# Layer 2's time mixing as a pipeline of four parts instead of two halves

## The reference

```python
h = layer_norm(x, ln1_g, ln1_b)
k = time_shift(h, mix_k) @ Wk_t.T
v = time_shift(h, mix_v) @ Wv_t.T
r = jax.nn.sigmoid(time_shift(h, mix_r) @ Wr_t.T)
wkv_out, new_state = wkv(-exp(time_decay), time_first, k, v)
x = x + r * wkv_out                      # time mixing
h2 = layer_norm(x, ln2_g, ln2_b)
kc = time_shift(h2, cmix_k) @ Wk_c.T     # 128 -> 512
rc = jax.nn.sigmoid(time_shift(h2, cmix_r) @ Wr_c.T)
vv = jnp.square(jax.nn.relu(kc)) @ Wv_c.T
x = x + rc * vv                          # channel mixing
```

## Time and profile before

| | |
|---|---|
| timed runs | 2173.11, 2174.31, 2175.66 us; median 2174.31 |
| profiled execution | 2182.17 us, span 2180.4 us |
| TensorE, VectorE, ScalarE, GpSimd busy | 1875.8 (86%), 1526.5 (70%), 1310.5 (60%), 588.6 us (27%) |
| chain that ended last | PE 52%, DVE 28%, ACT 8% |

### The profile page before, as it was taken

How to read it: one execution, slowest core, us unless ns; L and a number is a source line. 1 busy time by engine, 2 the same in 40 slices (tenths; PEclk the granted TensorE clock), 3 DMA queues, 4 the chain that set the end, 5 groups by cost and what they waited for, 6 DMA issues and landing times.

```text
span 2180.4 us, 37976 instructions
## 1 busy us (share of the span) xinstructions
PE 1875.8 (86%) x13416; PEld 1265.7 (58%) x13416; DVE 1526.5 (70%) x3631; ACT 1310.5 (60%) x2803; POOL 588.6 (27%) x569
## 2 busy tenths in 40 slices
PE   7999776997999999968977488999997997779886
PEld 4777564445777777644444254666665676534465
DVE  5777677866777677547848848899997456678533
ACT  5777533775878888735765656776665212357622
POOL 3223003102544443414001003444343001221043
PEclk9999997998999999978998699999999998889898
DMA  4000003411000000006302000000001000363202
GB/s 202 2 2 2 1 1 119 138 55 39 1 2 1 1 1 1 1 15 196 102 1 80 0 1 1 1 1 1 1 2 39 20 1 1 117 180 112 59 25 80
DMA packets 80156, 87.40 MB, mean 40 GB/s; under 512 B 6579, under 2 KB 70116, under 8 KB 79074
## 3 DMA queue, kind: packets, MB, share of 16 engines
q1 hardware_dynamic: 78625, 82.49, 11.9%
q0 software_dynamic: 1344, 2.49, 0.4%
HBM read 54.39 MB, written 30.70 MB: 39 GB/s over the span
## 4 chain that ended last, share of the span: by engine, by line
PE 52%; DVE 28%; ACT 8%; issue 6%; POOL 3%; DMA 2%; SPq 1%; DVEq 0%; POOLq 0%; ACTq 0%
PE bank L469 44%; DVE scratch L1269 4%; PE bank L653 2%; ACT XN L2059 2%; DVE scratch L3134 2%; DVE scratch L3154 2%; PE bank L3016 2%; PE bank L368 2%; PE bank L693 1%; DVE stats L245 1%; DVE XN L3174 1%; DVE scratch L1671 1%; DVE w_keep L1958 1%; ACT L2137 1%; PE bank L1238 1%
## 5 line engine op out<-in xcount | busy, mean ns | idle before, releaser
L469 PE MATMUL bank<-scratch 64*128 64x256 bf16 (+6 forms) x2936 | 307.7, 303 | 34.5 <-DMA scratch<-parts 13.5
L1269 DVE TENSOR_REDUCE scratch<-bank 128x2 f32<-128x512 f32 x384 | 243.1, 685 | 59.8 <-PE bank L469 59.2
L469 PE MATMUL bank<-w_keep,scratch 128*128 128x128 f32 (+4 forms) x1760 | 243.1, 329 | 19.2 <-DVE scratch L2001 4.0
L469 PEld LDWEIGHTS bank<-scratch 64*128 64x128 bf16 (+4 forms) x2936 | 177.3, 123 | 139.0 <-DVE scratch L1269 44.6
L1355 ACT ACTIVATE w_keep<-bank 128x512 f32<-128x512 f32 x384 | 212.4, 597 | 71.3 <-PE bank L469 63.6
L469 PE MATMUL bank<-XNT,w_keep 128*128 128x256 f32 (+4 forms) x800 | 236.9, 435 | 6.5 <-POOL w_keep L2198 5.5
L469 PEld LDWEIGHTS bank<-w_keep,scratch 128*128 128x128 f32 (+3 forms) x1760 | 181.7, 184 | 84.0 <-issue 54.8
L469 PE MATMUL bank<-w_early,scratch 64*128 64x256 f32 (+3 forms) x1152 | 163.3, 344 | 24.0 <-ACT w_early L3234 8.7
L469 PEld LDWEIGHTS bank<-XNT,w_keep 128*128 128x128 f32 x800 | 149.7, 196 | 58.0 <-issue 28.3
L469 PEld LDWEIGHTS bank<-w_early,scratch 64*128 64x128 f32 (+3 forms) x1152 | 119.0, 183 | 69.1 <-issue 28.5
L469 PE MATMUL bank<-w_keep 128*32 128x256 f32 (+2 forms) x1728 | 141.0, 389 | 13.3 <-ACT w_keep L1355 5.4
(11 more groups left out here) (461 smaller groups left out, 3852.0 us busy)
## 6 DMA issues: line engine op xcount, KB each, us to landing
scratch<-parts SPq DMA_DIRECT2D x24, 1024.0 KB, 5.2
parts<-scratch SPq DMA_DIRECT2D x192, 96.0 KB, 2.8
parts<-scratch SPq DMA_DIRECT2D x96, 64.0 KB, 2.1
w_early<-pack_l3f SPq DMA_DIRECT2D x1, 5206.0 KB, 15.4
w_keep<-pack_l2f SPq DMA_DIRECT2D x1, 2124.0 KB, 13.3
...
```

Source lines behind the costliest of these rows:

```text
L469: return pe.matmul(out, lhsT, rhs, start=start, stop=stop, skip_group_check=True)
L1269: dve.tensor_reduce(neg[:, :, h], self.compare_bank(g)[:, :].rearrange("p (t s) -> p t s", s=S), AXX, ALU.max, negate=True).then_inc(*s.ma ...
```

## The change

The pair of halves becomes a pipeline of four. A part has its own residual (`residual_dve`), moments (`moments_dve`, four tiles), norm (`norm_dve` and `norm_act`: two tiles scaled by each engine), turn (`turn_part_pe`) and affine step (`second_affine_dve`); the end of a quarter is `output_dve`. VectorE starts part 2's and part 3's first step later, and takes sums of a later part, weigh of the next, and gate of the current one in turn. ScalarE does the sigmoids of r in the middle of part 0's and part 1's work. TensorE makes the r products ahead of the v products of parts 1 to 3, and from there on turn, up, the next part's num, down for each part. The receptance sigmoids of quarters 0 and 1 are followed by one more load of the Ln and Exp table, and quarter 2's by one more load of the sigmoid table. The banks of num and turn are other ones.

The diff, cut to the functions and orders that the prediction speaks of:

```diff
@@ time_mixing @@
-    PARTS, FIRST, LAST = range(4), (0, 1), (2, 3)
-    num_bank = lambda part: k.bank[4 + part if part in FIRST else part]
+    PARTS = range(4)
+    num_bank = lambda part: k.bank[(4, 5, 2, 3)[part]]
+    turn_bank = lambda part: k.bank[(0, 3, 2, 3)[part]]
...
+    def norm_dve(dve, part):
+        tiles = slice(4 * part, 4 * part + 4)
+        total = k.moments[:, 1, tiles]
+        dve.wait_ge(*s.deviation.at("second", part))
+        dve.scalar_tensor_tensor(out=total, in0=total, scalar=-0.5, in1=k.rs[:, tiles], op0=ALU.mult, op1=ALU.mult).then_inc(*s.rstd.up("second", part))
+        dve.wait_ge(*s.rstd.at("second", part))
+        for i in range(4 * part, 4 * part + 2):
+            dve.tensor_scalar(O2[:, i], k.XN[:, i], k.rs[:, i:i + 1], k.moments[:, 1, i:i + 1], ALU.mult, ALU.add).then_inc(*s.normed.up("second", i))
...
@@ pe @@
...
-        for part in (0, 1):
-            num_pe(e, part)
-        turn_half_pe(e, "second", (0, 1))
-        e.wait_ge(*s.formed.at("second", 1))
-        up_pe(e, 0)
-        down_pe(e, 0)
-        num_pe(e, 2)
-        num_pe(e, 3)
-        up_pe(e, 1)
-        turn_half_pe(e, "later", (2, 3))
-        down_pe(e, 1)
-        e.wait_ge(*s.formed.at("later", 3))
-        for q in (2, 3):
+        for part in PARTS:
+            input_pe(e, part, 0)
+        input_pe(e, 0, 1)
+        for part in PARTS:
+            input_pe(e, part, 2)
+        for part in PARTS[1:]:
+            input_pe(e, part, 1)
+        num_pe(e, 0)
+        for q in PARTS:
+            turn_part_pe(e, q)
             up_pe(e, q)
+            if q + 1 in PARTS:
+                num_pe(e, q + 1)
             down_pe(e, q)
+
+    def input_pe(pe, part, n):
+        _, now, prev, _ = folded[INPUTS[n][0]]
+        bank, b0 = k.bank[part], part * PART
+        if n == 1:
+            pe.wait_ge(*s.stacked.at("in", part, 2 if part else 0))
+        elif n == 2:
+            pe.wait_ge(*s.stacked.at("in", part, 0 if part else 1))
...
@@ dve @@
...
+        ahead_dve(e, 0)
+        ahead_dve(e, 1)
+        sums_dve(e, 0)
+        raised_dve(e, 0)
+        ahead_dve(e, 2)
         level_dve(e, 0)
+        sums_dve(e, 1)
+        weigh_dve(e, 0)
+        whole_dve(e, 0)
+        raised_dve(e, 1)
+        gate_dve(e, 0)
+        ahead_dve(e, 3)
+        level_dve(e, 1)
+        residual_dve(e, 0)
         sums_dve(e, 2)
+        moments_dve(e, 0)
+        weigh_dve(e, 1)
+        norm_dve(e, 0)
+        whole_dve(e, 1)
+        second_affine_dve(e, 0)
...
+        residual_dve(e, 2)
+        moments_dve(e, 2)
         weigh_dve(e, 3)
+        norm_dve(e, 2)
+        whole_dve(e, 3)
+        second_affine_dve(e, 2)
+        gate_dve(e, 3)
+        output_dve(e, 0)
+        residual_dve(e, 3)
+        moments_dve(e, 3)
+        output_dve(e, 1)
+        norm_dve(e, 3)
+        second_affine_dve(e, 3)
+        output_dve(e, 2)
+        output_dve(e, 3)
@@ act @@
...
+        input_act(e, 0, 0)
+        input_act(e, 1, 0)
         weights_act(e, "first", 0)
+        input_act(e, 2, 0)
+        weights_act(e, "first", 1)
         input_act(e, 3, 0)
-        weights_act(e, "first", 1)
+        log_act(e, 0)
         input_act(e, 0, 1)
+        weights_act(e, "second", 0)
+        weights_act(e, "third", 0)
         weights_act(e, "first", 2)
...
         inverse_act(e, 0)
         for part in PARTS:
             input_act(e, part, 2)
         e.preload_act_table_set("natural_log_exp_and_others")
+        log_act(e, 1)
+        weights_act(e, "second", 1)
+        input_act(e, 1, 1)
+        weights_act(e, "third", 1)
+        norm_act(e, 0)
...
+        weights_act(e, "second", 3)
+        relu_act(e, 7)
+        norm_act(e, 2)
         weights_act(e, "third", 3)
         inverse_act(e, 3)
+        receptance_act(e, 0)
+        receptance_act(e, 1)
+        e.preload_act_table_set("natural_log_exp_and_others")
+        relu_act(e, 8)
+        relu_act(e, 9)
+        norm_act(e, 3)
+        relu_act(e, 10)
+        relu_act(e, 11)
+        receptance_act(e, 2)
```

More of the change, by code:

```diff
@@ L2625, in gate_dve, with residual_dve @@
         dve.tensor_tensor(num, num, r, ALU.mult).then_inc(*s.divided.up("gated", part))
[L2627 to L2642, removed]
+    def residual_dve(dve, part):
+        xn = k.XN[:, 4 * part:4 * part + 4, :]
+        dve.wait_ge(*s.rolled.at("num", part))
+        if part == 0:
+            dve.wait_ge(*s.scaled.at("outer", NT - 1))
+        dve.tensor_tensor(xn, xn, num_bank(part)[:, :].rearrange("p (j d) -> p j d", d=D), ALU.add).then_inc(*s.added.up("num", part))
+        dve.wait_ge(*s.added.at("num", part))
+        stats_dve(k, dve, "second", k.XN, range(4 * part, 4 * part + 4))
@@ new lines, in moments_dve @@
+    def moments_dve(dve, part):
+        tiles = slice(4 * part, 4 * part + 4)
+        m0, m1, v0, v1 = (k.stats[:, tiles, n] for n in (1, 4, 2, 5))
+        spread, total, var = (k.moments[:, n, tiles] for n in range(3))
+        dve.wait_ge(*s.stats.at("second", 4 * part + 3))
+        dve.tensor_tensor(spread, m0, m1, ALU.subtract).then_inc(*s.moments.up("spread", part))
+        dve.tensor_tensor(total, m0, m1, ALU.add).then_inc(*s.moments.up("total", part))
+        dve.tensor_tensor(var, v0, v1, ALU.add).then_inc(*s.moments.up("sums", part))
+        dve.wait_ge(*s.moments.at("spread", part))
+        dve.tensor_tensor(spread, spread, spread, ALU.mult).then_inc(*s.moments.up("square", part))
+        dve.wait_ge(*s.moments.at("square", part))
+        dve.scalar_tensor_tensor(out=var, in0=spread, scalar=P / 4, in1=var, op0=ALU.mult, op1=ALU.add).then_inc(*s.variance.up("second", part))
@@ new lines, in second_affine_dve, with output_dve @@
+    def second_affine_dve(dve, part):
+        dve.wait_ge(*s.turned.at("second", part))
+        dve.tensor_scalar(HT[:, 2 * part:2 * part + 2, 1:PADDED], turn_bank(part)[:, :].rearrange("p (b s) -> p b s", s=S), w["r_g2"], w["r_b2"],
+                          ALU.mult, ALU.add).then_inc(*s.formed.up("second", part))
+    def output_dve(dve, q):
+        tiles = k.X[:, 4 * q:4 * q + 4, :]
+        dve.wait_ge(*s.gated.at("rc", q))
+        dve.wait_ge(*s.multiplied.at("vv", q))
+        dve.tensor_tensor(RC[q % 2], RC[q % 2], k.bank[4 + q % 2][:, :], ALU.mult).then_inc(*s.vector.up("product", q))
+        dve.wait_ge(*s.vector.at("product", q))
+        dve.wait_ge(*s.pool.at("residual", q))
+        dve.tensor_tensor(tiles, tiles, RC[q % 2].rearrange("p (j d) -> p j d", d=D), ALU.add).then_inc(*s.added.up("out", q))
+        dve.wait_ge(*s.added.at("out", q))
+        stats_dve(k, dve, "next", k.X, range(4 * q, 4 * q + 4))
@@ L2696, in up_pe @@
             bank = k.bank[u % 2]
+            if g == 0:
+                pe.wait_ge(*s.formed.at("second", q))
             if u >= 2:
@@ L2759, in dve @@
-        affine_dve(e, "later", "r_g2", "r_b2", LAST)
-        for q in range(QUARTERS):
-            tiles = k.X[:, 4 * q:4 * q + 4, :]
-            e.wait_ge(*s.gated.at("rc", q))
-            e.wait_ge(*s.multiplied.at("vv", q))
-            e.tensor_tensor(RC[q % 2], RC[q % 2], k.bank[4 + q % 2][:, :], ALU.mult).then_inc(*s.vector.up("product", q))
-            e.wait_ge(*s.vector.at("product", q))
-            e.wait_ge(*s.pool.at("residual", q))
-            e.tensor_tensor(tiles, tiles, RC[q % 2].rearrange("p (j d) -> p j d", d=D), ALU.add).then_inc(*s.added.up("out", q))
-            e.wait_ge(*s.added.at("out", q))
-            stats_dve(k, e, "next", k.X, range(4 * q, 4 * q + 4))
+        residual_dve(e, 1)
```

118 lines of the change are left out of this document (48 added, 70 removed).

## The result

In nine runs the changed kernel took a median of 2185.32 us (2181.80 to 2190.07); nine runs of the kernel before on the same chip took 2175.66 (2171.66 to 2180.01). The ratio is **1.0045 (95% interval 1.0034 to 1.0056)**, 9.8 us slower (7.4 to 12.2). On the median of 2174.31 that the prediction started from, this is 2184.1 us.

A forecast was written before the change was run, and what follows sets the result against it. Two loads, TensorE's and VectorE's, stood one behind the other. Walking the in-order queues ended the stage at 1297.1 instead of 1290.45, 6.7 us longer; 2174.3 + 6.7 = 2181.0 us, range 2175.5 to 2187.5.

The forecast's parts named there:

- rival B: Clock also lost before value products and up 2, last up starting cold: +13.5, halved +10; 2184 to 2188 us; chance 0.16.
- r0: VectorE can add part 0's num at 1210.2, num queued behind value products that wait for sigmoids; 2.2 us lost.
- r1: VectorE can add part 1's num at 1230.3, after a cold first up of 9.2 us; 3.1 us lost.
- r2: VectorE can add part 2's num at 1246.3, after a warm up of 8.75 us with receptance; VectorE waits 2.7.
- r3: VectorE can add part 3's num at 1266.3, after warm up 2 (8.75) and relu 8's hold (1.3); 5.1 us waited.
- U3: Start of part 3's up, the last, on TensorE: 1282.1, behind down 2, turn and affine.
- Down 2: TensorE's second last down, waiting for squares until 1274.8 and starting cold: 5.9 us, all warm 3.7.
- The end: From residual 3 to last statistics: output 1, norm, relus 10 and 11, down 2, last up in series; ends 1297.1, before 1290.45.
- Rival A: TensorE warm throughout, up 0 and down 2 at high clock: 2.2 off twice, +2.3, 2176.6 us; chance 0.12.
- C: Engine loads set the end, VectorE's five waits (15.8 us) vanish: 2165.2 us, 0.4% faster; chance 0.08.
- Costs at nothing: 12 more small VectorE operations of the moments lie in its waits; without that cover 1 to 2 us.
- Table loads: On ScalarE, 1.29 us each up to the next operation, no drain; by the skill page some 4 us longer.

The follow-up runs named there:

- x5: Changed kernel with the old projection order on TensorE (k, v, r) and r products in banks 4 to 7: stage 114.0 us, ratio 1.0021.
- x3: Changed kernel plus matrix products nobody reads in TensorE's idle stretches (7 after num 0, 2 after turn 2, 8 after num 3): stage 110.6 us, ratio 1.0013.
- x1: Changed kernel with relu 10 and 11 ahead of norm 3 on ScalarE: stage 109.8 us, ratio 1.0014.
- x2: Changed kernel with quarter 1's output behind norm 3 and affine 3 on VectorE: stage 114.7 us, ratio 1.0031.
- x4: Changed kernel with the next part's num among the products of up on TensorE instead of behind them: stage 110.8 us, ratio 1.0004.
- x7: Changed kernel with the edits of x1, x2, x4 and x5 together: stage 99.5 us, ratio 0.9964.
- x9: x7 plus idle products after num 0 and turn 2, and ScalarE's third weights of part 3 between norm 2's root and scaling: stage 97.1 us, ratio 0.9958.

## Why the prediction was right, and what it mis-sized

The prediction was slower with 0.72, 2181.0 us, range 2175.5 to 2187.5: direction and range held. The size did not: it forecast +6.7 us, the stage shows +9.1 and the ratio +9.8, outside the forecast's own range (up to 2183.5) and at the lower end of rival B. The mechanism was right in the main, and its signs came: three last residuals that waited for num (3.3, 2.8, 6.5 us for 3, 3, 5), whole 3 waiting for ScalarE, 8.3 us of TensorE's time lost ahead of down 2, half clock in it, five table loads. Steps, in us after the first scan, as walked and as measured:

| step | walked | measured |
|---|---|---|
| residual 0 (r0) | 27.8 | 28.0 |
| residual 1 (r1) | 47.9 | 48.7 |
| residual 2 (r2) | 63.9 | 64.7 |
| residual 3 (r3) | 83.9 | 86.0 |
| last up (U3) | 99.7 | 102.1 |
| end | 114.7 | 117.2 |

- **r0.** Right to 0.2 us, with its cause: x5 takes it away.
- **r1, 0.8 late.** Up 0 was taken as cold, 9.2 for 9.60 measured. Turn 0 was priced warm, some 0.6 us; it was the first work after 6.84 us of idleness and took 1.16.
- **r3, another 1.2 late: the step that failed.** The prediction gave up 2 a warm 8.75 and 1.3 us of hold by relu 8 behind the two table loads. Measured, up 2 was cold, 9.85 for 7.14, and the hold didn't occur: relu 9, just behind relu 8, itself waited 1.60 us for TensorE. So +2.7 stood where +1.3 was summed. The idleness of 3.38 us ahead of up 2 was in the walk (whole 3's wait for third 3), but the clock was applied to the two longest pauses only. Rival B had named this one, at 0.9 us. x3 confirms the other half: warm up 2, and the hold appears at 1.21.
- **Down 2.** 6.50 for the estimate of 5.9. The clock rose late, 5.6 us after the work began where 4.4 was taken:

```profile
1282.00:1282.50 0.50, 0.50 (x5) 0.50 (x4) 0.00 (x0) 0.00 (x0) 0.00 (x0) 0.55 0.00 0
```

- **The end.** ScalarE's order as the cause of down 2's lateness: x1, -7.4 us. VectorE's output 1: x2, -2.5. The single gains add up to more than the loss of 9.1, so they aren't shares of it: an edit can also take out waits that the change didn't add. Those of x1, x2, x4 (as measured, with its cold value products) and x5 add up to 19.5 us, and together, in x7, they gave 17.7.
- **Rival B.** Of the 6.8 us that it adds to the forecast the profile shows some 2.0: 1.4 at up 2 (2.7 of cold for 1.3 of hold) and 0.6 at down 2. The value products and the last up stayed warm (5.42 and 7.14 us). That its halved sum, +10, is near the measured +9.1 to +9.8 is partly luck. The Trainium skill was cited for it ("TensorE: Matmul & The Clock Gate", Why this matters for your kernels): gaps bring the half clock back. The trace agrees at the r products behind 3.55 us of idleness, up 2 behind 3.38, turn 0 and up 0 behind 6.84 and down 2 behind 8.29; behind 2.65 us (value products) and 0.91 (last up) the clock stayed up.
- **Rival A and C.** A is out for the change; x3 shows what it would be (110.6). C is out for the change but not for a pipeline of four: x7 lies 8.6 us under the kernel before, and C, with all five waits gone, had 9.1. x9 is at 97.1 us, with TensorE busy 85.0 of 97.2, the idle products included.
- **Costs at nothing.** Small VectorE operations: 1.6 us more of busy time. Residual 3 with its moments took 2.39 us for the 2.49 walked, so where they stand on the chain they cost no more than was summed. No run took them out; that the others cost nothing is argued, not shown.
- **Table loads.** After one, the next activation came 1.29 us later (1257.04 to 1258.33), as in the earlier trace rows. The drain that the Trainium skill adds to it ("ScalarE: Activation LUTs", What ACT_TABLE_LOAD costs) did not show: the load itself takes 1.28.
- **8 us for profiling, "the same for both".** Not borne out. The profiled executions of the change and of x1 to x9 count among the timed runs of their kernels and lie anywhere among them (second lowest of eight for x7, highest of ten for x4), so no steady cost of profiling shows. Why before's was 8 us above its median stays open, since the remote wait was in the profiles of x1 to x9 too. It did no harm, since the difference was taken inside the stage; a difference of the two spans would have said "no change".
